# A window-attention pipeline: another order of the matmuls within a step, and outputs one step earlier

## The reference, cut to what matters

```python
DIM, DEPTH, HEADS, DIM_HEAD, WINDOW = 128, 6, 16, 64, 32     # x is (2, 1024, 128)
def attn_layer(x, Wqkv, qs, ksc, Wo):
    q, k, v = (sh(t) for t in jnp.split(x @ Wqkv, 3, -1))
    q, k = l2norm(q) * qs, l2norm(k) * ksc
    q = q * cos * scale + rotate_half(q) * sin * scale
    k = k * cos * inv + rotate_half(k) * sin * inv
    # each window of 32 queries sees its own 32 keys and the 32 before, masked to a band
    sim = jnp.einsum('bhwie,bhwje->bhwij', bq, bk2) * QK_SCALE
    attn = jax.nn.softmax(jnp.where(mask, -big, sim), -1)
    out = jnp.einsum('bhwij,bhwje->bhwie', attn, bv2)
    return out @ Wo
for i in range(DEPTH):
    x = attn_layer(shift_tokens(x), ...) + x
    x = ffn_layer(shift_tokens(x), ...) + x        # layernorm, (a * gelu(gate)) @ W2
```

## Time and profile before

| what | us |
|---|---|
| three timed runs: median (lowest to highest) | 2413.82 (2401.31 to 2416.41) |
| the profiled execution: its own time, its span | 2405.99, 2404.1 |
| PE busy, DVE, ACT, POOL | 2066.7, 1774.6, 1492.8, 1256.0 |

### The profile page before, as it was taken

The page is one execution under the profiler, slowest core; times in us unless marked ns, Lnnn a source line. Parts: engine busy times, 40 slices in busy tenths (PEclk is TensorE's granted clock), DMA queues, the critical chain, the costliest instruction groups (busy, mean ns, idle before and its releaser), DMA issues. The chain is left out here.

```text
span 2404.1 us, 81162 instructions
## 1 busy us (share of the span) xinstructions
PE 2066.7 (86%) x33532; PEld 1431.0 (60%) x33532; DVE 1774.6 (74%) x3984; ACT 1492.8 (62%) x5170; POOL 1256.0 (52%) x869
## 2 busy tenths in 40 slices
PE   5549999899999999989999999999999964763377
PEld 2337767576675766747667576675766732432255
DVE  4669779597795977959779597795977836685754
ACT  2239769497785976849769497684876823451122
POOL 1138668386783857838678386783865701221000
PEclk8679999999999999999999999999999985885699
DMA  2011111111111111111111111111110100001000
GB/s 96 0 36 41 30 31 54 38 44 30 33 53 37 46 28 35 51 37 44 30 35 53 35 44 30 34 51 38 40 30 25 42 1 12 1 0 54 1 0 17
DMA packets 86557, 80.34 MB, mean 33 GB/s; under 512 B 15040, under 2 KB 82624, under 8 KB 85568
## 3 DMA queue, kind: packets, MB, share of 16 engines
q1 hardware_dynamic: 86208, 75.37, 10.9%
HBM read 25.51 MB, written 1.05 MB: 11 GB/s over the span
## 5 line engine op out<-in xcount | busy, mean ns | idle before, releaser
L984 POOL TENSOR_TENSOR RN<-N,minus_half 128x8 f32<-128x8 f32 x384 | 632.6, 1648 | 158.1 <-DVE N L916 157.1
L822 ACT ACTIVATE PB<-PS,NMX 128x64 f32<-128x64 f32 x1536 | 461.9, 312 | 126.2 <-DVE NMX L950 126.0
L663 PE MATMUL PS<-WQ,XS 128*128 128x256 f32 x1536 | 398.7, 383 | 13.9 <-SPq L538 13.0
L822 ACT ACTIVATION_READ_ACCUMULATOR PB<-PS,NMX 128x1 f32 x1536 | 311.1, 203 | 0.0
L979 POOL TENSOR_TENSOR RR<-R1B,R 128x512 f32<-128x512 f32 x192 | 244.4, 1273 | 103.8 <-DVE QK L940 103.8
L979 POOL TENSOR_TENSOR RR<-R 128x512 f32<-128x512 f32 x192 | 245.4, 1278 | 97.7 <-DVE QK L940 97.7
L663 PEld LDWEIGHTS PS<-WQ,XS 128*128 128x128 f32 x1536 | 264.1, 192 | 35.3 <-SPq L538 13.3
L916 DVE TENSOR_REDUCE N<-SQ 128x8 f32<-128x512 f32 x384 | 259.4, 675 | 5.5 <-ACT SQ L810 5.4
L933 DVE TENSOR_TENSOR R<-PS,SINL 128x512 f32<-128x512 f32 x384 | 262.0, 682 | 1.0 <-POOL RR L979 1.0
L940 DVE SCALAR_TENSOR_TENSOR QK<-RN,RR 128x512 f32<-128x512 f32 x384 | 261.2, 680 | 0.0
L650 PE MATMUL PS<-ident,QK 128*128 128x128 f32 x1536 | 252.1, 287 | 1.8 <-DVE QK L940 1.8
(11 more groups left out here) (210 smaller groups left out, 3582.9 us busy)
## 6 DMA issues: line engine op xcount, KB each, us to landing
VS<-XB SPq DMA_DIRECT2D x384, 96.0 KB
VS<-XB SPq DMA_DIRECT2D x288, 32.0 KB
WQ<-in_wqkv SPq DMA_DIRECT2D x40, 192.0 KB, 2.4
WO<-in_wo SPq DMA_DIRECT2D x6, 512.0 KB, 3.7
BIG<-in_wgu SPq DMA_DIRECT2D x1, 2048.0 KB, 8.7
W<-in_w SPq DMA_DIRECT2D x6, 341.0 KB, 4.0
WQ<-in_wqkv SPq DMA_DIRECT2D x1, 1536.0 KB, 12.0
QKS<-in_qks SPq DMA_DIRECT2D x6, 256.0 KB, 3.4
```

Of the source, the lines that this page charges most:

```text
L663: mm = nc.tensor.matmul(PQ[:, (g + 3) % 2, j * 256:(j + 1) * 256], XSb[b][:, t0:t0 + P], WQ[:, pair * 384:pair * 384 + 256], start=True, s ...
L822: ex = nc.scalar.activation(PB[:, g % 2, u, :], SC[:, h, DH * t:DH * t + DH], ACT.Exp, bias=NMX[:, u:u + 1], accum_out=PSUMS[:, g % 2, u:u ...
L984: nc.gpsimd.tensor_tensor(RN[:, g % 2, :], N2[:, g % 2, :], minus_half[:, :], ALU.pow)
```

## The change

PE's order within a step becomes P, T, B, V, M, S, O. O is that of chunk g-2 instead of g-3, from the `XB` copy that ACT makes in the same step, so its wait for `vp_in` now stands in front of it at the end of the step. ACT's order becomes QKT, XB, SQ, OTS, E. DVE's becomes R1, N2, RO, R2, PB (of g-1 instead of g-2), NMX, QK. The feed-forward moves from g % 32 == 2 to 1, its last product from bank 3 to 7, and `ffn_pe` is waited for before O. The matmuls and their sizes are the same.

```diff
-                return (k // B, k % B) if k >= 0 and g % SLOT == 2 else None
+                return (k // B, k % B) if k >= 0 and g % SLOT == 1 else None
...
-            WOUT, TOKS, FEAT, DOWN = (6, 7), (2, 5), (6, 7), (5, 3)
+            WOUT, TOKS, FEAT, DOWN = (6, 7), (2, 5), (6, 7), (5, 7)
...
@@ tensor: step(g)
-                        if there(g):
-                            pe.wait_ge(qk_in.sem, qk_in.take())
...
-                            tr.then_inc(qkt_ps.sem, 1)
                         if there(g + 3):
...
                             mm.then_inc(proj_in.sem, 1)
-                        if there(g) or there(g - 3):
-                            pe.wait_ge(vp_in.sem, vp_in.take())
                         if there(g):
-                            pe.sem_inc(v_in.sem, 1)
-                        if there(g - 3):
-                            c = (g - 3) % CH
-                            if g - 3 > 0:
-                                pe.wait_ge(o_free.sem, o_free.take())
...
-                        if feed_forward_at(g - 1):
-                            pe.wait_ge(ffn_pe.sem, ffn_pe.take())
-                        if there(g):
...
+                            pe.wait_ge(qk_in.sem, qk_in.take())
+                            for k in range(2):
+                                for j in range(CB):
+                                    tr = nc.tensor.transpose(TQ[:, (2 * k + j) * P:(2 * k + j + 1) * P],
+                                                             QK[:, g % 2, j, k, :], ident[:, :])
+                            tr.then_inc(qkt_ps.sem, 1)
                         if probs:
                             pe.wait_ge(vs_in.sem, vs_in.take())
                             pe.wait_ge(pn_in.sem, pn_in.take())
...
                             last.then_inc(vp_ps.sem, 1)
                         if there(g):
                             c = g % CH
+                            if g > 0:
+                                pe.wait_ge(sc_free.sem, sc_free.take())
...
+                        if there(g):
+                            c = g % CH
                             pe.wait_ge(qkt_in.sem, qkt_in.take())
...
                             mm.then_inc(sc_in.sem, 1)
+                        if values or probs:
+                            pe.wait_ge(vp_in.sem, vp_in.take())
+                        if values:
+                            pe.sem_inc(v_in.sem, 1)
+                        if feed_forward_at(g - 1):
+                            pe.wait_ge(ffn_pe.sem, ffn_pe.take())
+                        if probs:
+                            c = (g - 2) % CH
+                            if g - 2 > 0:
+                                pe.wait_ge(o_free.sem, o_free.take())
...
+                                            XB[keys, (g + 1) % CH, cols:cols + WIN],
+                                            start=True, stop=True)
+                            mm.then_inc(o_ps.sem, 1)
                         if ffn:
-                            if values or probs:
-                                pe.wait_ge(vp_in.sem, vp_in.peek(1))
                             pe.wait_ge(o_free.sem, o_free.peek(1))
                             feed_forward(*ffn, g)
@@ scalar: step(g)
-                        if there(g - 3):
-                            l, b, pair, c = where(g - 3)
+                        if values or probs:
+                            cols = slice(0 if values else 256, 512 if probs else 256)
+                            act.wait_ge(vp_ps.sem, vp_ps.take())
+                            nc.scalar.activation(XB[:, (g + 1) % CH, cols], PX[:, cols], ACT.Copy)\
+                                .then_inc(vp_in.sem, 1)
...
+                        if there(g - 2):
+                            l, b, pair, c = where(g - 2)
                             act.wait_ge(o_ps.sem, o_ps.take())
@@ vector: step(g)
+                        k = (g - 1) % 2
+                        if there(g - 1):
+                            dve.wait_ge(sc_free.sem, g)
+                            nc.vector.reciprocal(RO[:, k, :], PSUMS[:, k, :]).then_inc(ro_in.sem, 1)
```

More of the change, by code:

```diff
@@ L717, in step @@
                             c = g % CH
+                            if g > 0:
+                                pe.wait_ge(sc_free.sem, sc_free.take())
+                            for h in range(2):
+                                nc.tensor.matmul(
+                                    SC[:, h, 0:P], identb[:, :],
+                                    bandmask[:, 0 if c == 0 else 1, :, :].rearrange("p t k -> p (t k)"),
+                                    start=True, stop=False)
+                        if there(g):
+                            c = g % CH
                             pe.wait_ge(qkt_in.sem, qkt_in.take())
@@ L799, in step @@
                                 TQ.rearrange("p (k s) -> p k s", k=2), ACT.Copy).then_inc(qkt_in.sem, 1)
-                        if there(g - 3):
-                            l, b, pair, c = where(g - 3)
+                        if values or probs:
[3 more added lines that the diff above has]
+                                .then_inc(vp_in.sem, 1)
+                        if there(g + 3):
+                            act.wait_ge(proj_in.sem, proj_in.take())
+                            nc.scalar.activation(SQ[:, (g + 3) % 2, :, :].rearrange("p g d -> p (g d)"),
+                                                 PQ[:, (g + 3) % 2, :], ACT.Square).then_inc(sq_in.sem, 1)
+                        if there(g - 2):
+                            l, b, pair, c = where(g - 2)
                             act.wait_ge(o_ps.sem, o_ps.take())
@@ L807, in step @@
                                 .then_inc(o_free.sem, 1)
[L808 to L816, removed]
                         if there(g):
@@ L937, in step @@
                                 .then_inc(rot_in.sem, 1)
[L938 to L943, removed]
[L944 to L947 removed]
+                        if there(g - 1):
+                            dve.wait_ge(ro_in.sem, ro_in.take())
+                            nc.vector.tensor_tensor(
+                                PB[:, k, :, :], PB[:, k, :, :],
+                                RO[:, k, :].unsqueeze(2).to_broadcast([P, 4, 2 * WIN]), ALU.mult)\
+                                .then_inc(pn_in.sem, 1)
                         if there(g):
```

44 lines of the change are left out of this document (17 added, 27 removed).

## The result

| | before | after |
|---|---|---|
| timed runs, same chip: median (lowest to highest), us | 2412.14 (2401.31 to 2416.41) | 2461.00 (2454.46 to 2461.49) |
| the profiled execution: own time, span | 2405.99, 2404.1 | 2454.46, 2452.6 |

The ratio is 1.0213, 95% interval 1.0188 to 1.0237: the change makes the kernel 2.1% slower. The sum had given 2453 for the profiled execution.

The account below looks back on a forecast made before the run. The prediction took a PE and DVE ring of 3.46 us per step as the bound; a new ring of 3.59 over 361 plain steps added 47 us to 2406, giving 2453, range 2405 to 2490.

Parts of the forecast that it names:

- Bound of before: Plain step: ring S, NMX, N2, R1, PB, B, V over PE and DVE, 3.46 us; PE's own slack about 0.12.
- What is removed: Both old rings cut, and three changes of tile size per step instead of four, 0.10 us for the one saved.
- Neither ring: The old bound S, NMX, N2, R1, PB, B, V of 3.46 us, and close behind it NMX, E, M.
- What is added: O waits for the same step's XB, closing a new ring of 3.59 us; +47 us over 361 plain steps.
- The forecast's ring: P, T, B, V, XB, O and back to P, all PE but for ACT's XB: 3.59 us; chance 0.62 for 3.53 to 3.65.
- XB's end to O: Handover from ACT's finished copy to PE's O, taken as 0.12 us, between 0.05 and 0.14 seen elsewhere.
- The other rings: ACT 3.35 us, DVE with POOL 3.40, DVE alone 3.23; all below 3.59, so none decides.
- The feed-forward: Twelve times: project starts 1.23 us later, NMX behind it 0.81 sooner; taken as nothing in all, 5 us either way.
- PE's own work: Rival: XB's wait is covered, PE needs 3.25 us, DVE and POOL's 3.40 binds, 2384 us; chance 0.10.
- A ring no longer than the old one: Rival: P's weight load hidden and O waking in 0.05 give 3.42 us; either alone 2417 to 2428; chance 0.20.
- O starting cold: Rival: O's 64 loads and passes behind a wait cost 0.15 us more per step, 3.74, 2507 us; chance 0.08.
- The signs: Next profile: intervals 3.5 to 3.65 us, PE idle about 0.3 before O as longest wait, P's load open, clock full.

Follow-up runs that it names:

- e5: Kernel before with only DVE's order changed, to N2, R1, QK, RO, R2, PB (of g-1), NMX; 2362.50 us, ratio 0.9839.
- e8: e7 with DVE's order changed to N2, R1, QK, RO, R2, PB, NMX; 2358.56 us, ratio 0.9808 to the kernel before.
- e3: Changed kernel with ACT doing the squares SQ before the copy XB; 2575.3 us in its one run, step 3.92.
- e1: Changed kernel, but O is again of chunk g-3, reading the previous step's XB copy (eight slots); 2404.52 us, ratio 0.9986 to the kernel before.
- e4: Changed kernel with DVE's QK moved before RO; 2461.92 us, ratio 1.0235 to the kernel before, step 3.61.
- e7: e1 with PE raising v_in earlier, between T and B; 2395.57 us, ratio 0.9965 to the kernel before.
- e10: e7 with SP's wait for the next layer's WQ moved behind the shifted values; 2370.94 us, ratio 0.9872 to the kernel before.
- e11: Changed kernel with v_in raised behind O and o_free waited for before vp_in; 2451.89 us, ratio 1.0205 to the kernel before.
- e6: e8 with PE's O placed between T and B, giving four changes of tile size; 2417.94 us, ratio 1.0061 to the kernel before.
- e9: e8 with SP's wait for the next layer's WQ moved behind the shifted values; 2323.86 us, ratio 0.9672 to the kernel before.
- e2: e1 with DVE's QK moved before RO; 2393.71 us, ratio 0.9940 to the kernel before, steps 3.12 and 3.48.

## Why the prediction was right

**Bound of before: right.** e5, which moves only DVE's order and so cuts that ring, gives 3.33: PE's old order had 0.13 of slack; I had said 0.12. M's two matmuls, put at 0.11, take 0.12 there.

**What is removed: right.** Neither ring holds PE in after. Its two orders differ by 0.07 (e5 and e8), which the links add up: 0.10 for the fourth change of size and 0.05 for T's first load, open behind S (T to P 0.49, T to B 0.44), less the 0.10 by which P's open load makes the new order longer, and 0.02 in M to B and B to V. P's first load stood open as I had it: P to T took 0.97 in after and in e8, with no change of size in it. After a feed-forward, where P follows matmuls of the full size, it took 0.86:

```profile
942.69 1.03 PE L656 MATMUL PS<-WQ,XS 128*128 128x256 f32 x4
943.55 0.60 PE L665 MATMUL PS<-ident,QK 128*128 128x128 f32 x4
```

By the rule of the Trainium skill, TensorE: Matmul & The Clock Gate, part 2, a load is pulled ahead where the row groups do not conflict or the background weight buffer takes it. Had it been so here, the link would be 0.87; behind O it is not.

**What is added: right, with one term a little small.** The forecast's ring is in the trace, link by link. The mis-sized term is XB's end to O, 0.12 forecast and 0.145 measured; with roundings of 0.01 on the other links the ring is 3.61 where I had 3.59. e3 shows the ring by lengthening it, e1 by cutting it, e4 that DVE's side does not matter. The idle time before O was 0.33 forecast and is 0.28 to 0.29 in the view, which counts from the modelled end of S. From start to start, S to O takes 0.74 in after and 0.38 in e8: the wait costs 0.36.

**The other rings: right.** DVE with POOL was put at 3.40 and binds at 3.41 once PE's ring is gone (e1, e7, e10). ACT's ring of 3.35 binds in none of the runs, so its sum is not tested.

**The feed-forward: right in its terms, with luck in the sum.** Its project starts 1.25 later (1.23 forecast), and NMX behind it comes after 2.19 (2.30 forecast). An undisturbed interval grew by 0.22 where I had 0.42. In sum, the intervals that hold or follow one gave back 1.2 us; I had taken nothing, and that it came out so near is in part the odd long ones named above.

**The rivals.** PE's own work: its 3.25 is real (e8), but the wait for XB was not covered. A ring no longer than the old one: both of its conditions failed, the load stood open and O woke in 0.145, even with a single wait (e11). O starting cold did not happen: its first eight matmuls start at 957.99 and its last eight from 958.33, and P follows at 0.60 from O's start, as before.

**The signs.** As the longest entry among the waits I had named PE's O. It is the longest of PE's, but POOL, ACT and DVE have longer ones, which hold nothing up.

The total: 361 x 0.138 = +49.7 less 1.2, against a forecast of +47. The plain steps alone would give 361 x 0.146 = +52.7. The profiled execution was forecast at 2453 and was 2454.46; the median of all runs, 2461.0, lies 6.5 over it and within the range.

## What to carry to other kernels

Before an operation is moved closer to the step that makes its input, add up the ring that it closes: producer, copy, handover and every instruction queued between the consumer and the next producer on the same engine. Here it was 3.59 against 3.46, readable from rows of before, and regrouping could pay only with the input left a step old. What it then pays depends on the order that it replaces: 0.15 per step of PE's own work against e6, but 0.07 against before's order (e5), so that most of the 3.3% of e9 comes from DVE's order and SP's. When a step gets shorter, look at the queues that were in time only by the slack of the old step: one wait of SP in the wrong place cost 29 us (the profiled executions of e8 and e9).

## What was not expected of the hardware

POOL's RN, always the same form, took two durations in e2. Timeline of e2, POOL:

```profile
1017.82 2.03 POOL L984 TENSOR_TENSOR RN<-N,minus_half 128x8 f32<-128x8 f32 x1 [1.94 <-DVE N L923]
...
1021.08 1.65 POOL L984 TENSOR_TENSOR RN<-N,minus_half 128x8 f32<-128x8 f32 x1
```

and of DVE:

```profile
1017.65 0.68 DVE L928 SCALAR_TENSOR_TENSOR QK<-RN,RR 128x512 f32<-128x512 f32 x1
...
1021.12 0.70 DVE L928 SCALAR_TENSOR_TENSOR QK<-RN,RR 128x512 f32<-128x512 f32 x1
```

e2 is e1 with QK before RO.

```diff
@@ vector: step(g), order
-R1, N2, RO, R2, PB, NMX, QK
+R1, N2, QK, RO, R2, PB, NMX
```

> As the kernel with outputs of three steps ago in the changed order, and on DVE the scaled queries and keys QK of g+1 go from the end of the step to the place before RO: R1, N2, QK, RO, R2, PB, NMX, with the wait for RR before QK. Theory: now the ring of DVE and POOL is cut as well (RR has from R2 of one step to QK of the next), and PE's own work is the bound: 0.97 + 0.44 + 0.22 + 0.44 + 0.11 + 0.10 + 0.28 + 0.10 + 0.60, a plain step of 3.26 us, with PE never waiting; 361 x -0.35 = -126 us against the changed kernel, about 2335, 3% below the kernel before. Rival (PE needs more per step than the sum of its parts, or DVE's own 3.23 with its waits is the bound): 3.40 or more, 2385 or more.

The ring N2, RN, RR, QK binds there, and the plain steps alternate between 3.12 and 3.48, 3.30 in the mean, where 3.26 was expected. The median came to 2394 and not to the 2335 expected, 11 us under e1 instead of 50; PE also stands longer for the shifted values (47.2 us against 32.1).

Here RN took 2.03 when POOL had stood idle before it, and 1.65 right behind RR. But the idle time is not the condition: in e6 it took 1.65 after idle time too, 358 times. Timeline of e6, POOL:

```profile
959.01 1.65 POOL L984 TENSOR_TENSOR RN<-N,minus_half 128x8 f32<-128x8 f32 x1 [0.16 <-DVE N L918]
```

What goes with the long ones is their start within DVE's QK. Over the traces of all 13 kernels, all 578 RN that start while DVE is in QK took 2.0 or more (209 in e2, 369 in e4), and none of the 4414 others did, such as that at 1021.08, 0.04 before QK. The nearer the start to that of QK, the longer: 0.17 after it RN is 0.37 longer, and in the one that starts 0.03 after it 0.52. Both come to 0.54 after QK's start.

RR shows the same beside PB. Timeline of e8, DVE and POOL:

```profile
673.14 0.41 DVE L944 TENSOR_TENSOR PB<-PB,RO 128x256 f32<-128x256 f32 x1
673.30 1.38 POOL L979 TENSOR_TENSOR RR<-R1B,R 128x512 f32<-128x512 f32 x1 [0.21 <-DVE R L937]
```

All 1481 RR that start 0.15 to 0.20 after PB took some 1.38, where the earlier trace rows has 1.27; the 219 that start later in PB did not lengthen so. QK and PB are DVE's two instructions of a step with both inputs in SBUF; R1 and R2 have one in PSUM, and under them RR took 1.27. So it reads as if POOL stood until DVE had gone through 0.54 of QK or 0.27 of PB. That is inferred from starts and durations; no run changes this alone.

The intervals with a feed-forward are longer in e8 and e9 (41.7 and 41.8 in the mean) than in e10 (40.6). About half of it is P's wait for DVE's R2: 11.1 us in 14 times in e8 and e9, 4.2 us in 8 times in e10. The rest is open.
